# Cross, linear and one-head attention: the projection's tiles run inside the normalisation's block, each waiting for its chunk of 512 tokens

## Chip, cores and metric

One core of one Trainium2 chip runs the whole program. The metric is the device time of one execution in microseconds (us). TensorE is written PE, its weight loads PEld, VectorE DVE, ScalarE ACT, GpSimd POOL and SyncE SP.

## What is computed

Two decoder layers work on x of 2 x 1024 tokens x 256 features, each sublayer in the form `x = x + f(layernorm(x))`. The change touches the second, fourth and fifth of the six sublayers:

```
layernorm(x) = (x - mean(x)) / sqrt(var(x) + 1e-5)          # over the 256 features
x = x + cross(layernorm(x), ctx)      # 16 heads, q = xn @ Wq.T, k, v from 77 context rows per batch
x = x + linear(layernorm(x))          # q, k = relu(...), v; sum over tokens of k v, then q times that
x = x + one_head(layernorm(x), ctx)   # xp = relu(xn @ W.T + b), yp = relu(ctx @ W.T + b), softmax(xp yp), times ctx
```

All of it is float32.

## The kernel before

The 2048 tokens (N) lie along the free dimension and the 256 features on 128 partitions in C = 2 halves, so X and XN are tiles of 128 x 2 x 2048. Work on tokens goes in NCH = 4 chunks of W = 512. The kernel is a sequence of blocks. A block holds an instruction list for each engine; inside it engines wait only for each other's semaphores, and at its end all engines meet in a barrier, which the order below prints as two branches, the second of which waits for the release.

`norm` (L91) is one such block. PE multiplies a chunk by a matrix of 1/256 for the mean (L132, PSUM banks 0 to 3), DVE subtracts it (L152, signal `centred`), ACT squares (L184), PE forms the variance (L139, banks 4 to 7), ACT takes the reciprocal root with its square and its half (L188, L191, L193), DVE refines it (L159, signal `newton`, and L163, signal `rstd_ready`), and the chunk is scaled: chunks 0 and 1 by POOL (L225, signal `scaled`), 2 and 3 by DVE (L168, signal `scaled_dve`). The parameters of the sublayer are loaded by SP in the same block (signal `moved`).

`project` (L264) is a block that works through a list of `Tile`s: for tile n, PE sums the tile's products in bank n % 8 (L290, signal `summed`), and the tile's engine, ACT or DVE, takes the bank out to SBUF (L335, L339, L1756, L1881; signals `taken_act` and `taken_dve`). From the ninth tile on PE first waits until the tile eight places earlier has been taken. `steps` (L342) is a block for a chain of small operations, here fills of constants (L1275, L1769, L1870) and the two operations that make a mask (L1876, L1878).

The three sublayers `cross` (L1261), `linear` (L1738) and `cross_one` (L1858) each begin with `norm`, then have the projections of XN and the context in one `project`, in `cross` and `cross_one` with a block of `steps` between the two, in `linear` behind them. Cross has 14 tiles: 8 of q (512 columns, two products each), 4 of k (77 columns) and 2 of v. Linear has 16 pairs of k and v tiles (256 columns) and 8 of q. One-head has 8 tiles of xp (512 columns) and 2 of yp (154 columns). Each product appears in the trace as two matmul instructions.

Of the kernel before, what the change touches and what calls it, by code (L numbers as in the profile page):

```python
# [15 lines left out]
P = 128  # L16
B, T, D = 2, 1024, 256
N = B * T
# [25 lines left out]
class Signal:  # L44


    def __init__(self, sem):
        self.sem, self.base = sem, 0
# [39 lines left out]
    moved.passed(16 * len(pairs))  # L88


def norm(k, src, dst, centre=True, eps=EPS, weight=None, bias=None, loads=(), later=(), later_in=None, fills=()):  # L91

# [5 lines left out]
    var_ready, root_ready, root_squared = k.sig("var_ready"), k.sig("root_ready"), k.sig("root_squared")  # L98
    newton, halved, rstd_ready = k.sig("newton"), k.sig("halved"), k.sig("rstd_ready")
    scaled, scaled_dve, normed, filled = k.sig("scaled"), k.sig("scaled_dve"), k.sig("normed"), k.sig("filled")  # L100
    affine = weight is not None
    with ExitStack() as ctx:

# [74 lines left out]

        @block.scalar
        def _(act):  # L180
# [30 lines left out]
            if affine:  # L211
                for c in range(NCH):
                    affine_chunk(c)

        @block.gpsimd
        def _(pool):
# [24 lines left out]
    if loads:  # L241
        moved.passed(16 * len(loads))
    filled.passed(len(fills))


class Tile:

    def __init__(self, products, engine, take, rows=P, cols=W, then=None):  # L250
        self.products, self.engine, self.take, self.rows, self.cols = products, engine, take, rows, cols
        self.then = then


class Pending:
# [8 lines left out]
def project(k, tiles, banks=8, pending=None, beside=()):  # L264
# [15 lines left out]
    with nc.Block() as block:  # L280
# [53 lines left out]
def copy_to(dst, func=ACT.Copy, scale=1.0):  # L334
    return lambda eng, bank: eng.activation(dst, bank, func, scale=scale)  # L335
# [925 lines left out]
def cross(k, a):  # L1261

    X = k.X
    with ExitStack() as ctx:
        XN = k.sb("XN", [P, C, N], ctx=ctx)
        w = [k.sb(n, [P, C, D], ctx=ctx) for n in ("wq", "wk", "wv", "wo")]
        cx = k.sb("cx", [P, C, B * S2], ctx=ctx)
        norm(k, X, XN, loads=[(cx[:], a["ctx"])] + [(t[:], a["cross_" + n]) for t, n in zip(w, "qkvo")])
        recip = k.sb("recip", [P, B * CPB * C, W], ctx=ctx)
        jobs, tiles = [], []  # L1270
        for b in range(B):
            kk = k.sb("kk", [P, C, S2], ctx=ctx)
            v = k.sb("v", [P, 1, D], ctx=ctx)
            jobs.append(Job(k.sb("q", [P, C, T], ctx=ctx)[:], kk[:], v, X[:, :, b * T:(b + 1) * T]))
        steps(k, "chain", [("dve", lambda e, job=job: e.memset(job.v[:], 0.0)) for job in jobs])  # L1275
        for b, job in enumerate(jobs):
            for m in range(C):
                cols = slice(m * P, (m + 1) * P)
                for h in range(CPB):
                    prods = [(w[0][:, c, cols], XN[:, c, b * T + h * W:b * T + (h + 1) * W]) for c in range(C)]  # L1280
                    tiles.append(Tile(prods, "act", copy_to(job.q[:, m, h * W:(h + 1) * W])))
                prods = [(w[1][:, c, cols], cx[:, c, b * S2:(b + 1) * S2]) for c in range(C)]
# [455 lines left out]
def linear(k, a):  # L1738

    nc, ps, X = k.nc, k.ps, k.X  # L1740
    with ExitStack() as ctx:
# [5 lines left out]
        norm(k, X, XN, loads=[(w[:], a["lin_qkv"]), (wo[:], a["lin_proj"]), (bias[:], a["lin_bias"]),  # L1747
                              (same[:], a["same_head"])])
# [3 lines left out]
        vt = k.sb("lv", [P, N // P, D], ctx=ctx)  # L1752
        tiles = []
        for t in range(N // P):
            prods = [(XN[:, c, t * P:(t + 1) * P], w[:, c, D:3 * D]) for c in range(C)]
            tiles.append(Tile(prods, "act", lambda e, bank, t=t: e.activation(kt[:, t, 0:D], bank[:, 0:D], ACT.Relu)))  # L1756
            tiles.append(Tile([(XN[:, c, t * P:(t + 1) * P], w[:, c, 2 * D:3 * D]) for c in range(C)], "dve",
                              dve_copy_to(vt[:, t, :]), cols=D))
            tiles[-2].cols = D
            tiles[-2].products = [(l, r[:, 0:D]) for l, r in prods]  # L1760
# [7 lines left out]
        ones = k.sb("lones", [P, P], ctx=ctx)  # L1768
        steps(k, "chain", [("dve", lambda e: e.memset(ones[:], 1.0))])  # L1769
        tiles = []  # L1770
        for b in range(B):
            for c in range(C):
# [85 lines left out]
def cross_one(k, a):  # L1858
# [3 lines left out]
    with ExitStack() as ctx:  # L1862
# [5 lines left out]
        mask_in = k.sb("mask_in", [P, B, S2], I32, ctx=ctx)  # L1868
        mask = k.sb("mask", [P, B, S2], ctx=ctx)
        steps(k, "chain", [("dve", lambda e: e.memset(ct[:], 0.0))])  # L1870
        norm(k, X, XN, loads=[(w[:], a["one_w"]), (bias[:], a["one_bias"]), (cx[:], a["ctx"]),
                              (ct[0:S2, :, :], a["ctx_rows"])]
             + [(mask_in[:, b, :], a["mask"][b:b + 1, :].broadcast_to([P, S2])) for b in range(B)])
        yp = k.sb("yp", [P, C, B * S2], ctx=ctx)
        xp = k.sb("xp", [P, C, N], ctx=ctx)
        steps(k, "chain", [("dve", lambda e: e.tensor_copy(mask[:], mask_in[:])),  # L1876

                           ("dve", lambda e: e.tensor_scalar(mask[:], mask[:], -3e38, 10.0, ALU.mult, ALU.mult))])  # L1878
        tiles = []
        for m in range(C):  # L1880
            relu = lambda dst, m: (lambda e, bank: e.activation(dst, bank, ACT.Relu, bias=bias[:, m:m + 1]))  # L1881
            tiles.append(Tile([(w[:, c, m * P:(m + 1) * P], cx[:, c, :]) for c in range(C)], "act",
                              relu(yp[:, m, :], m), cols=B * S2))
            for h in range(NCH):
                prods = [(w[:, c, m * P:(m + 1) * P], XN[:, c, h * W:(h + 1) * W]) for c in range(C)]
                tiles.append(Tile(prods, "act", relu(xp[:, m, h * W:(h + 1) * W], m)))
# [5 lines left out]
        for h in range(NCH):  # L1892
            b = h // CPB
            for g in range(G):
# [4 lines left out]
        project(k, tiles)  # L1899
# [235 lines left out]
```

## Time and profile before

| | |
|---|---|
| time, median of 3 runs | 2994.42 us (2988.17 to 2995.18) |
| the profiled execution's own time | 2993.08 us |
| its span in the trace | 2990.6 us |
| granted PE clock, mean of the span | 0.923 of full speed |
| PE, DVE, ACT, POOL busy | 79%, 65%, 60%, 44% of the span |

The median is 1.34 us above the profiled execution, and the three runs lie within 7 us of each other. Busy shares are means over six sublayers with different limits; most of the span is the first sublayer. The three places that the change touches lie at 1555 to 1600 us (cross), 2641 to 2711 us (linear) and 2757 to 2800 us (one-head) of the span.

### The profile page before, as it was taken

What the parts mean: (1) busy time and instruction counts of PE and PEld (TensorE: products, weight loads), DVE (VectorE), ACT (ScalarE), POOL (GpSimd) and SP (SyncE); (2) the same over time, 40 slices, a digit from 0 to 9 for tenths busy, and PEclk for the clock granted to TensorE, in tenths of its full rate; (3) what the DMA queues carried; (4) which work ended last, traced back from release to release, by engine and by line L of the source; (5) the groups of instructions that cost most, each with busy time, mean ns of one, the idle gap of its engine ahead of it and who ended that gap; (6) DMA issues with size and microseconds to landing.
All of it is one profiled execution on the core that took longest, in us unless ns stands there. A gap on an engine that the chain in (4) does not pass through costs nothing. (4 is left out here: it accounts for less than half of the span.)

```text
span 2990.6 us, 38704 instructions
## 1 busy us (share of the span) xinstructions
PE 2374.3 (79%) x12420; PEld 1200.4 (40%) x12421; DVE 1957.9 (65%) x1762; ACT 1794.5 (60%) x2789; POOL 1311.3 (44%) x492
## 2 busy tenths in 40 slices
PE   5688888888868888888877667797787499868778
PEld 2344444444334444444435123223222355545333
DVE  4699999999669999999964657515913122233440
ACT  4799999999479999999951440270064211122330
POOL 2089998999508999999951110000000300020000
PEclk8899999999989999999996889898889699979889
DMA  2320001000133000100000400010012400010000
GB/s 77 90 76 28 25 29 39 28 25 28 41 88 77 28 25 29 39 28 28 25 20 3 113 36 1 9 40 11 1 34 88 174 21 21 20 43 9 28 0 28
DMA packets 59817, 116.17 MB, mean 39 GB/s; under 512 B 13619, under 2 KB 21811, under 8 KB 58304
## 3 DMA queue, kind: packets, MB, share of 16 engines
q1 hardware_dynamic: 51104, 103.72, 11.0%
q0 software_dynamic: 8608, 11.05, 1.3%
q8 instruction: 65, 1.06, 0.1%
q14 instruction: 40, 0.33, 0.0%
HBM read 86.92 MB, written 27.53 MB: 38 GB/s over the span
## 5 line engine op out<-in xcount | busy, mean ns | idle before, releaser
L838 POOL TENSOR_TENSOR hs<-hs,c_bc 128x2048 f32<-128x2048 f32 x256 | 1166.3, 4556 | 63.9 <-DVE hs L889 48.6
L889 DVE TENSOR_TENSOR_SCAN hs<-decays,ps 128x512 f32<-128x512 f32 x512 | 610.8, 1215 | 26.4 <-PE ps L916 8.0
L889 DVE TENSOR_TENSOR_SCAN hs<-decays,carry,ps 128x512 f32<-128x512 f32 x512 | 621.7, 1270 | 8.5 <-PE ps L916 7.7
L924 PE MATMUL ps<-hs,sel 128*64 128x512 f32 x2048 | 498.4, 608 | 15.4 <-POOL hs L838 15.1
L916 PE MATMUL ps<-ident,dbu_even 128*128 128x128 f32 x2048 | 294.9, 283 | 94.8 <-DVE hs L889 65.8
L916 PE MATMUL ps<-ident,dbu_odd 128*128 128x128 f32 x2048 | 294.9, 283 | 91.5 <-DVE hs L889 60.5
L852 ACT ACTIVATE decays<-delta_far,A 128x512 f32<-128x512 f32 x512 | 358.2, 712 | 10.3 <-DVE hs L889 10.2
L852 ACT ACTIVATE decays<-delta_near,A 128x512 f32<-128x512 f32 x512 | 356.4, 707 | 3.2 <-DVE hs L889 3.2
L860 ACT ACTIVATE dbu_odd<-du_turned,b_turned 128x512 f32<-128x512 f32 x512 | 357.1, 710 | 0.0
L860 ACT ACTIVATE dbu_even<-du_turned,b_turned 128x512 f32<-128x512 f32 x496 | 346.0, 710 | 0.0
L916 PEld LDWEIGHTS ps<-ident,dbu_odd 128*128 128x128 f32 x2048 | 221.1, 142 | 241.4 <-DVE hs L889 188.0
L916 PEld LDWEIGHTS ps<-ident,dbu_even 128*128 128x128 f32 x2048 | 219.0, 141 | 245.4 <-DVE hs L889 196.1
L1071 ACT ACTIVATE prob<-ps 128x1024 f32<-128x1024 f32 (+2 forms) x224 | 176.0, 837 | 161.5 <-PE ps L1042 137.5
L924 PEld LDWEIGHTS ps<-hs,sel 128*64 128x64 f32 x2048 | 124.6, 136 | 213.0 <-issue 186.4
L994 POOL DMA_DIRECT2D q<-o_rows x13 | 9.1, 698 | 401.5 <-DMA o_rows<-osb 336.8
L1196 PE MATMUL ps<-kx,qx 32*128 32x77 f32 (+4 forms) x1280 | 135.7, 545 | 55.9 <-DVE negmax L1223 33.0
L1080 DVE COPY osb<-ps 128x512 f32<-128x512 f32 x32 | 21.8, 690 | 215.3 <-PE ps L1053 213.3
L1223 DVE TENSOR_REDUCE negmax<-ps 128x4 f32<-128x2048 f32 (+4 forms) x70 | 138.8, 2028 | 22.6 <-PE ps L1201 14.9
L1627 PE MATMUL ps<-w_wv,x_turned 128*128 x304 | 141.2, 608 | 10.7 <-ACT x_turned L1686 10.7
L1722 DVE TENSOR_SCALAR hid_turned<-ps 128x512 f32<-128x512 f32 x38 | 26.3, 691 | 178.6 <-PE ps L1635 178.6
L1036 PE MATMUL ps<-qx,kx 32*128 32x512 f32 (+4 forms) x896 | 112.4, 572 | 38.7 <-PEq L1244 20.4
L1384 POOL DMA_INDIRECT rows<-ys,slot x16 | 15.2, 949 | 249.3 <-ACTq L1380 244.7
(260 smaller groups left out, 2664.3 us busy)
## 6 DMA issues: line engine op xcount, KB each, us to landing
c_bc<-c_rows SPq DMA_DIRECT2D x256, 128.0 KB, 2.8
o_rows<-osb SPq DMA_DIRECT2D x32, 256.0 KB
u_rows<-u SPq DMA_DIRECT2D x4, 1024.0 KB, 4.5
d_rows<-delta SPq DMA_DIRECT2D x4, 1024.0 KB, 4.2
delta_near<-d_rows SPq DMA_DIRECT2D x4, 1024.0 KB, 9.8
hs<-u_rows SPq DMA_DIRECT2D x4, 1024.0 KB, 6.5
delta_far<-d_rows SPq DMA_DIRECT2D x4, 1024.0 KB, 12.1
w_down<-in_expert_proj SPq DMA_DIRECT2D x1, 4096.0 KB, 36.6
```

The lines of the kernel that those rows point to most:

```text
L838: pool.tensor_tensor(x, x, spread(c_bc[:, g, :], 4), ALU.mult).then_inc(weighed.sem, 1)
L852: act.activation(decays[:, s % RING, :], (far if q else near)[:, blk, :], ACT.Exp, scale=A[:, at(i * GB, g), blk]).then_inc(decay.sem, 1)
L860: act.activation(dbu[0], dbu[1], ACT.Copy, scale=dbu[2]).then_inc(made.sem, 1)
L889: dve.tensor_tensor_scan(hs[:, quad % RING, n, :], decays[:, s % RING, :], ps[:, DBU + s % RING, :], carry[:, at(i * GB, g), blk] if q els ...
L916: mm = pe.transpose(ps[:, DBU + s % RING, t * P:(t + 1) * P], room[g % 2][:, t, blk, :, :].rearrange("p n d -> p (n d)"), k.ident[:])
L924: mm = pe.matmul(ps[lo:lo + DB, ACC + quad % 2 * 2 + j // 2, :], k.sel2[:, :], hs[:, quad % RING, j, :], start=False, stop=False, skip_gro ...
L1036: mm = pe.matmul(ps[0:krows, 2 * (m % 3) + j % 2, first:W], job.kx[rows, par, c, t * P:t * P + krows], job.qx[rows, par, c, qc * W + first ...
L1071: act.activation(prob[0:krows, m % 4, :, first:W], ps[0:krows, 2 * (m % 3):2 * (m % 3) + 2, first:W], ACT.Exp).then_inc(weighed.sem, 1)
L1196: mm = pe.matmul(ps[:, STRIPS * (f % 2) + j, at:at + m], qx[strip, par, c, t * P:(t + 1) * P], kx[strip, par, c, o:o + m], start=True, sto ...
L1223: dve.tensor_reduce(to[:, :, groups[0]:groups[0] + per], banks[:, :, :, 0:m], AX.X, ALU.max, negate=True).then_inc(maxed.sem, 1)
L1627: mm = pe.matmul(ps[:, 2 * h + g, :], xt[:, p, c, :], wv[:, bass.ds(e * (C * 2 * FF) + (c * 2 * FF + g * FF + h * HALF), HALF)], start=(c ...
L1722: dve.tensor_scalar(hid_t[:, h, :, :], ps[:, HID + h, :].rearrange("p (f n) -> p f n", f=HT), 1.0, None, ALU.mult).then_inc(hid_copied.sem, 1)
```

## The change

The list of tiles is handed to `norm`, whose block now also does what `project` did. Behind its last variance, PE goes through the tiles; each tile of XN waits for the signal that its chunk (`chunk=`) is scaled, and the first eight tiles wait until the bank of a mean or of a variance has been read. ACT and DVE take the tiles out at the end of their own part of the normalisation. The tiles are ordered by chunk, and those of the context stand last. The fills of constants move ahead of `norm`; the two mask operations of one-head move into the later `project` of the scores, as operations that DVE does `beside` it. The core of the diff:

```diff
@@ norm, PE, behind the last variance
+            if tiles:
+                pe.wait_ge(moved.sem, moved.at(16 * len(loads)))
+            for n, t in enumerate(tiles):
+                if n < NCH:
+                    if centre:
+                        pe.wait_ge(centred.sem, centred.at(n + 1))
+                elif n < 2 * NCH:
+                    pe.wait_ge(newton.sem, newton.at(n - NCH + 1))
+                else:
+                    old = n - 2 * NCH
+                    pe.wait_ge(taken[tiles[old].engine].sem, taken[tiles[old].engine].at(count[old]))
+                if t.chunk is not None:
+                    if affine:
+                        pe.wait_ge(normed.sem, normed.at((t.chunk + 1) * C))
+                    elif t.chunk < BY_POOL:
+                        pe.wait_ge(scaled.sem, scaled.at(t.chunk + 1))
+                    else:
+                        pe.wait_ge(scaled_dve.sem, scaled_dve.at(t.chunk - BY_POOL + 1))
+                multiply(pe, ps, t, n % 8).then_inc(summed.sem, 1)
@@ norm, DVE, behind the last chunk; ACT alike
+            take_tiles(dve, "dve", k, tiles, count)
+def take_tiles(eng, name, k, tiles, count):
+    summed, taken = k.sig("summed"), k.sig("taken_" + name)
+    for n, t in enumerate(tiles):
+        if t.engine == name:
+            eng.wait_ge(summed.sem, summed.at(n + 1))
+            t.take(eng, k.ps[0:t.rows, n % 8, 0:t.cols]).then_inc(taken.sem, 1)
@@ project, DVE
+            if beside:
+                dve.wait_ge(went_by.sem, went_by.at(len(beside)))
             take_all(dve, "dve")
@@ cross
-        norm(k, X, XN, loads=[(cx[:], a["ctx"])] + [(t[:], a["cross_" + n]) for t, n in zip(w, "qkvo")])
...
         steps(k, "chain", [("dve", lambda e, job=job: e.memset(job.v[:], 0.0)) for job in jobs])
         for b, job in enumerate(jobs):
+            for h in range(CPB):
+                for m in range(C):
+                    prods = [(w[0][:, c, m * P:(m + 1) * P], XN[:, c, b * T + h * W:b * T + (h + 1) * W])
+                             for c in range(C)]
+                    tiles.append(Tile(prods, "act", copy_to(job.q[:, m, h * W:(h + 1) * W]), chunk=b * CPB + h))
...
-        project(k, tiles)
+        norm(k, X, XN, loads=[(cx[:], a["ctx"])] + [(t[:], a["cross_" + n]) for t, n in zip(w, "qkvo")], tiles=tiles)
@@ linear
+        steps(k, "chain", [("dve", lambda e: e.memset(ones[:], 1.0))])
         tiles = []
...
         for h in range(NCH):
+            for t in range(h * W // P, (h + 1) * W // P):
+                x = [XN[:, c, t * P:(t + 1) * P] for c in range(C)]
+                tiles.append(Tile([(x[c], w[:, c, D:2 * D]) for c in range(C)], "act",
+                                  copy_to(kt[:, t, 0:D], ACT.Relu), cols=D, chunk=h))
+                tiles.append(Tile([(x[c], w[:, c, 2 * D:3 * D]) for c in range(C)], "dve",
+                                  dve_copy_to(vt[:, t, :]), cols=D, chunk=h))
             for m in range(C):
                 prods = [(w[:, c, m * P:(m + 1) * P], XN[:, c, h * W:(h + 1) * W]) for c in range(C)]
-                tiles.append(Tile(prods, "act", copy_to(q[:, m, h * W:(h + 1) * W], ACT.Relu)))
-        project(k, tiles)
+                tiles.append(Tile(prods, "act", copy_to(q[:, m, h * W:(h + 1) * W], ACT.Relu), chunk=h))
+        norm(k, X, XN, loads=[(w[:], a["lin_qkv"]), (wo[:], a["lin_proj"]), (bias[:], a["lin_bias"]),
+                              (same[:], a["same_head"])], tiles=tiles)
@@ cross_one
+        for h in range(NCH):
+            for m in range(C):
+                prods = [(w[:, c, m * P:(m + 1) * P], XN[:, c, h * W:(h + 1) * W]) for c in range(C)]
+                tiles.append(Tile(prods, "act", relu(xp[:, m, h * W:(h + 1) * W], m), chunk=h))
+        for m in range(C):
+            tiles.append(Tile([(w[:, c, m * P:(m + 1) * P], cx[:, c, :]) for c in range(C)], "act",
+                              relu(yp[:, m, :], m), cols=B * S2))
...
-        project(k, tiles)
+        project(k, tiles, beside=[lambda e: e.tensor_copy(mask[:], mask_in[:]),
+                                  lambda e: e.tensor_scalar(mask[:], mask[:], -3e38, 10.0, ALU.mult, ALU.mult)])
```

What this does to PE's list in cross, where the normalisation ends and the projection begins, before the change (a row is one or more products; L139 is the variance, L290 a tile's product, and a signal in brackets is what the row waits for):

```order
L139 MATMUL ps<-norm_sq,inv 128x512 [waits squared]
L139 MATMUL ps<-norm_sq,inv 128x512
L230 UNCONDITIONAL_BRANCH
L281 UNCONDITIONAL_BRANCH [waits barrier_Pool_Activation_PE_DVE_SP_release]
L290 MATMUL ps<-XN,wq 128x512 x4
L290 MATMUL ps<-cx,wk 128x77 x2
L290 MATMUL ps<-XN,wq 128x512 x4
L290 MATMUL ps<-cx,wk 128x77 x2
```

And the same place of PE's list with the change (L141 is now the variance, L298 a tile's product):

```order
L141 MATMUL ps<-norm_sq,inv 128x512 [waits squared]
L141 MATMUL ps<-norm_sq,inv 128x512
L298 MATMUL ps<-XN,wq 128x512 [waits scaled,centred,moved]
L298 MATMUL ps<-XN,wq 128x512
L298 MATMUL ps<-XN,wq 128x512 [waits scaled,centred]
L298 MATMUL ps<-XN,wq 128x512
```

The two branches of the barrier are gone, and the first products of q follow the last variance; tiles 0 to 7 now carry two or three waits where they carried none.

In linear, PE's list around the ninth tile is this with the change (w_qkv,XN are tiles of k and v, XN,w_qkv those of q; the first two rows are the eighth tile, the third and fourth the ninth):

```order
L298 MATMUL ps<-w_qkv,XN 128x256 [waits scaled,newton]
L298 MATMUL ps<-w_qkv,XN 128x256
L298 MATMUL ps<-XN,w_qkv 128x512 [waits scaled,taken_act]
L298 MATMUL ps<-XN,w_qkv 128x512
L298 MATMUL ps<-XN,w_qkv 128x512 [waits scaled,taken_dve]
L298 MATMUL ps<-XN,w_qkv 128x512
L298 MATMUL ps<-w_qkv,XN 128x256 [waits scaled,taken_act]
L298 MATMUL ps<-w_qkv,XN 128x256
```

The tiles of q, which stood behind all of k and v, now stand behind each chunk's own, and from the ninth tile on PE waits for takes that ACT and DVE do only after their part of the normalisation.

On DVE the scores' block of one-head begins with the mask operations (L1953, L1954), ahead of the first score (L1951):

```order
L1953 CAST mask_192<-mask_in_191 128x154
L1954 TENSOR_SCALAR mask_192<-mask_192 128x154 [waits went_by]
L1951 TENSOR_TENSOR sc_200<-ps,mask_192 128x77 [waits summed,went_by]
L1951 TENSOR_TENSOR sc_200<-ps,mask_192 128x77 [waits summed] x15
```

Before, the two stood in a block of their own between the normalisation and the projection.

## Rows read from the trace of the kernel before

**Rows 1.** Timeline, around the cross projection: start us, us, engine, line, operation [idle before it <- releaser]
```profile
1554.50 0.69 DVE L1258 TENSOR_TENSOR X<-X,ps 128x512 f32<-128x512 f32 x1 [2.74 <-PE ps L290]
1555.82 3.67 PE L132 MATMUL ps<-X,inv 128*128 128x512 f32 x8 [1.35 <-PEq L280]
...
1569.71 1.98 PE L139 MATMUL ps<-norm_sq,inv 128*128 128x512 f32 x4 [0.69 <-ACT norm_sq L184]
...
1569.97 2.35 POOL L225 TENSOR_TENSOR XN<-XN,norm_rstd 128x1024 f32<-128x1024 f32 x1 [1.08 <-DVE norm_rstd L163]
...
1575.49 1.23 DVE L168 TENSOR_TENSOR XN<-XN,norm_rstd 128x1024 f32<-128x1024 f32 x1
1577.12 0.66 DVE L1275 MEMSET v<- 128x256 f32 x2 [0.40 <-PEq L230]
...
1578.32 6.41 PE L290 MATMUL ps<-XN,wq 128*128 128x512 f32 x8 [6.63 <-PEq L345]
```

**Rows 2.** Timeline, around the linear projection
```profile
2640.68 1.22 DVE L1403 TENSOR_TENSOR X<-X,ps 128x1024 f32<-128x1024 f32 x1 [3.75 <-PE ps L1394]
...
2642.22 5.24 PE L132 MATMUL ps<-X,inv 128*128 128x512 f32 x8 [1.58 <-PEq L1380]
...
2663.48 1.23 DVE L168 TENSOR_TENSOR XN<-XN,norm_rstd 128x1024 f32<-128x1024 f32 x1
2665.00 29.59 PEld L290 LDWEIGHTS ps<-w_qkv,XN 128*128 128x128 f32 x128 [6.15 <-issue]
2665.03 29.96 PE L290 MATMUL ps<-w_qkv,XN 128*128 128x256 f32 x128 [5.35 <-PEq L230]
...
2707.05 0.60 ACT L335 ACTIVATE lq<-ps 128x512 f32<-128x512 f32 x1 [1.12 <-PE ps L290]
...
2708.76 0.60 ACT L335 ACTIVATE lq<-ps 128x512 f32<-128x512 f32 x1 [1.12 <-PE ps L290]
...
2710.39 1.86 PEld L290 LDWEIGHTS ps<-lv,lk 128*128 128x128 f32 x16 [2.49 <-issue]
```

**Rows 3.** Timeline, around the one-head projection
```profile
2757.82 0.48 DVE L1870 MEMSET ct<- 128x512 f32 x1 [0.46 <-PEq L1788]
...
2758.85 3.67 PE L132 MATMUL ps<-X,inv 128*128 128x512 f32 x8 [2.27 <-PEq L345]
...
2780.34 0.24 DVE L1878 TENSOR_SCALAR mask<-mask 128x154 f32<-128x154 f32 x1
...
2781.11 1.36 PE L290 MATMUL ps<-cx,w_one 128*128 128x154 f32 x4 [6.39 <-PEq L345]
...
2782.51 0.39 ACT L1881 ACTIVATE yp<-ps,one_bias 128x154 f32<-128x154 f32 x1 [5.74 <-PE ps L290]
...
2798.26 0.69 ACT L1881 ACTIVATE xp<-ps,one_bias 128x512 f32<-128x512 f32 x1 [1.03 <-PE ps L290]
...
2799.25 7.34 PE L290 MATMUL ps<-yp,xp 128*128 128x77 f32 x64 [1.03 <-PEq L280]
2799.93 0.24 DVE L1897 TENSOR_TENSOR sc<-ps,mask 128x77 f32<-128x77 f32 x1 [19.35 <-PE ps L290]
```

**Rows 4.** Windows: stretch, us, busy us of each engine, granted clock, DMA share, GB/s
```profile
1555.80:1571.70 15.90, 14.51 (x32) 5.82 (x32) 8.16 (x9) 11.31 (x15) 4.08 (x2) 1.00 0.24 77
1578.30:1584.60 6.30, 6.28 (x9) 2.72 (x10) 0.00 (x0) 0.60 (x1) 0.00 (x0) 0.56 0.00 0
1584.60:1599.20 14.60, 13.86 (x49) 7.31 (x47) 1.80 (x6) 4.18 (x7) 0.00 (x0) 1.00 0.00 0
2665.00:2669.50 4.50, 4.47 (x11) 3.68 (x12) 0.42 (x1) 0.38 (x1) 0.00 (x0) 0.52 0.02 4
2669.50:2709.40 39.90, 39.22 (x151) 28.17 (x149) 6.36 (x15) 10.54 (x23) 0.00 (x0) 1.00 0.00 0
2781.10:2785.60 4.50, 4.49 (x9) 2.60 (x10) 0.00 (x0) 0.39 (x1) 0.00 (x0) 0.53 0.00 0
2785.60:2799.20 13.60, 12.62 (x33) 5.57 (x31) 0.00 (x0) 5.78 (x9) 0.00 (x0) 1.00 0.00 0
```

More of the change, by code:

```diff
@@ L88, in load, with norm @@
     moved.passed(16 * len(pairs))
-def norm(k, src, dst, centre=True, eps=EPS, weight=None, bias=None, loads=(), later=(), later_in=None, fills=()):
+def norm(k, src, dst, centre=True, eps=EPS, weight=None, bias=None, loads=(), later=(), later_in=None, fills=(),
+         tiles=()):
     nc, ps = k.nc, k.ps
@@ L100, in norm @@
     scaled, scaled_dve, normed, filled = k.sig("scaled"), k.sig("scaled_dve"), k.sig("normed"), k.sig("filled")
+    summed, taken, done, count = k.sig("summed"), signals_taken(k), *takes_of(tiles)
     affine = weight is not None
@@ L213, in _ @@
                     affine_chunk(c)
+            take_tiles(act, "act", k, tiles, count)
         @block.gpsimd
@@ L243, in norm, with __init__, signals_taken, takes_of @@
     filled.passed(len(fills))
+    summed.passed(len(tiles))
+    for name in taken:
+        taken[name].passed(done[name])
 class Tile:
-    def __init__(self, products, engine, take, rows=P, cols=W, then=None):
+    def __init__(self, products, engine, take, rows=P, cols=W, then=None, chunk=None):
         self.products, self.engine, self.take, self.rows, self.cols = products, engine, take, rows, cols
-        self.then = then
+        self.then, self.chunk = then, chunk
+def signals_taken(k):
+    return {"act": k.sig("taken_act"), "dve": k.sig("taken_dve")}
+def takes_of(tiles):
+    done = {"act": 0, "dve": 0}
+    count = []
+    for t in tiles:
+        done[t.engine] += 1
+        count.append(done[t.engine])
+    return done, count
+def multiply(pe, ps, t, bank):
+    for i, (lhs, rhs) in enumerate(t.products):
+        mm = pe.matmul(ps[0:t.rows, bank, 0:t.cols], lhs, rhs, start=(i == 0), stop=(i == len(t.products) - 1))
+    return mm
+def take_tiles(eng, name, k, tiles, count):
[4 more added lines that the diff above has]
+            t.take(eng, k.ps[0:t.rows, n % 8, 0:t.cols]).then_inc(taken.sem, 1)
 class Pending:
@@ L1276, in cross @@
         for b, job in enumerate(jobs):
-            for m in range(C):
[L1278 to L1282, printed above, removed]
+            for h in range(CPB):
[3 more added lines that the diff above has]
+                    tiles.append(Tile(prods, "act", copy_to(job.q[:, m, h * W:(h + 1) * W]), chunk=b * CPB + h))
+        for b, job in enumerate(jobs):
+            for m in range(C):
+                prods = [(w[1][:, c, m * P:(m + 1) * P], cx[:, c, b * S2:(b + 1) * S2]) for c in range(C)]
                 tiles.append(Tile(prods, "dve", dve_copy_to(job.kk[:, m, :]), cols=S2))
@@ L1746, in linear @@
         same = k.sb("same_head", [P, P], ctx=ctx)
-        norm(k, X, XN, loads=[(w[:], a["lin_qkv"]), (wo[:], a["lin_proj"]), (bias[:], a["lin_bias"]),
-                              (same[:], a["same_head"])])
         q = k.sb("lq", [P, C, N], ctx=ctx)
@@ L1752, in linear @@
         vt = k.sb("lv", [P, N // P, D], ctx=ctx)
+        ones = k.sb("lones", [P, P], ctx=ctx)
+        steps(k, "chain", [("dve", lambda e: e.memset(ones[:], 1.0))])
         tiles = []
[L1754 to L1760, printed above, removed]
-        for h in range(NCH):
+        for h in range(NCH):
+            for t in range(h * W // P, (h + 1) * W // P):
[4 more added lines that the diff above has]
+                                  dve_copy_to(vt[:, t, :]), cols=D, chunk=h))
             for m in range(C):
                 prods = [(w[:, c, m * P:(m + 1) * P], XN[:, c, h * W:(h + 1) * W]) for c in range(C)]
-                tiles.append(Tile(prods, "act", copy_to(q[:, m, h * W:(h + 1) * W], ACT.Relu)))
-        project(k, tiles)
+                tiles.append(Tile(prods, "act", copy_to(q[:, m, h * W:(h + 1) * W], ACT.Relu), chunk=h))
+        norm(k, X, XN, loads=[(w[:], a["lin_qkv"]), (wo[:], a["lin_proj"]), (bias[:], a["lin_bias"]),
+                              (same[:], a["same_head"])], tiles=tiles)
         ctxw = k.sb("ctxw", [P, B, C, P], ctx=ctx)
         ksw = k.sb("ksw", [P, B, C, P], ctx=ctx)
-        ones = k.sb("lones", [P, P], ctx=ctx)
-        steps(k, "chain", [("dve", lambda e: e.memset(ones[:], 1.0))])
         tiles = []
@@ L1870, in cross_one @@
         steps(k, "chain", [("dve", lambda e: e.memset(ct[:], 0.0))])
+        yp = k.sb("yp", [P, C, B * S2], ctx=ctx)
+        xp = k.sb("xp", [P, C, N], ctx=ctx)
+        relu = lambda dst, m: (lambda e, bank: e.activation(dst, bank, ACT.Relu, bias=bias[:, m:m + 1]))
+        tiles = []
+        for h in range(NCH):
[5 more added lines that the diff above has]
+                              relu(yp[:, m, :], m), cols=B * S2))
         norm(k, X, XN, loads=[(w[:], a["one_w"]), (bias[:], a["one_bias"]), (cx[:], a["ctx"]),
                               (ct[0:S2, :, :], a["ctx_rows"])]
[L1873 to L1886, printed above, removed]
-        project(k, tiles)
+             + [(mask_in[:, b, :], a["mask"][b:b + 1, :].broadcast_to([P, S2])) for b in range(B)], tiles=tiles)
         sc = k.sb("sc", [P, NCH, G, S2], ctx=ctx)
@@ L1898, in cross_one @@
                     sc[:, h, g, :], bank, mask[:, b, :], ALU.add), cols=S2))
-        project(k, tiles)
+        project(k, tiles, beside=[lambda e: e.tensor_copy(mask[:], mask_in[:]),
+                                  lambda e: e.tensor_scalar(mask[:], mask[:], -3e38, 10.0, ALU.mult, ALU.mult)])
         flat = sc[:].rearrange("p h g s -> p (h g) s")
```

## The prediction

> **What bounds the kernel now.** The busy shares of the page say little here, since they are a mean over six sublayers and the change touches some 160 us of 2990.6. I read the timeline around the three places first, then the windows, for the clock granted there. In each of the three the order is the same: PE ends the last variance, the normalisation's small operations on ACT, DVE and POOL go on, a barrier and in two of the three a block of fills or mask operations follow, and PE stands until the first tile. In cross PE's last variance begins at 1569.71 and ends 1.98 us later, at 1571.69; the next PE row is the first product of q at 1578.32, with 6.63 us idle before it [rows 1]. In linear the pause is 5.35 us [rows 2], in one-head 6.39 us [rows 3]. No other engine does anything in these pauses that the tiles need from outside the normalisation.
>
> After each pause the windows show the second loss: the granted clock is 0.56 over the first 6.30 us of the tiles in cross, 0.52 over the first 4.50 us in linear and 0.53 over 4.50 us in one-head, and 1.00 behind that. 0.5 is the lower of the two levels, 1.2 GHz, and 1.00 the upper, 2.4 GHz. Inside the cross normalisation, where PE is busy 14.51 of 15.90 us, the clock is 1.00 [rows 4].
>
> During the tiles PE is what everybody waits for: ACT waits 1.12 us for each q tile of linear and works 0.60 us, so a tile comes every 1.71 us (2707.05 to 2708.76) [rows 2].
>
> **What the change does, part by part.** *The pause.* With the change the first tile stands behind the last variance. Is its chunk ready by then? In cross, POOL's second chunk is scaled from 1569.97 to 1572.32 [rows 1]; it began 1.08 us after POOL's first chunk had ended, at 1568.89, so chunk 0 is ready 2.8 us before PE gets to tile 0 at 1571.69. At 1.71 us for a tile of 512 columns, PE comes to chunk 1 at 1575.1 (ready 1572.32) and to chunk 3, 6 x 1.71 us behind the start, at 1581.9; DVE's last scaling ends at 1576.72 [rows 1]. One-head runs the same normalisation with the same operations. In linear a chunk is eight tiles of 256 columns and two of 512, 10.3 us, so chunks are never waited for. Nothing else is late: all three pauses go. That is 6.63 + 5.35 + 6.39 = 18.4 us.
>
> *The banks.* Tile 7 waits for `newton` of chunk 3, which DVE gives before it begins its last scaling. In linear that begins at 2663.48 at the latest; PE, which would start at 2665.03 - 5.35 = 2659.68, has seven tiles of 0.86 us (half of 1.71) ahead of tile 7 and reaches it at 2665.7. Tile 9 is the first that needs a take of DVE, and DVE is free at 2663.48 + 1.23 = 2664.71 [rows 2], so tile 1 is taken by 2665.2; PE gets to tile 9 at 2659.68 + 8 x 0.86 + 1.71 = 2668.3. The slack is 2 to 3 us at each. This is where a small error would turn into a new wait, since a DVE instruction that waits there has all later v tiles queued behind it.
>
> *The ramp.* If PE goes on without a pause, the tiles begin at full clock. The lower clock now costs 6.30 x (1 - 0.56) = 2.77 us, 4.50 x 0.48 = 2.16 us and 4.50 x 0.47 = 2.12 us [rows 4], together 7.05 us.
>
> *The waits themselves.* Up to 56 tiles (8 in cross, 40 in linear, 8 in one-head) now carry two or three waits. In linear the tiles from the ninth on already carry one, for a take. The 128 weight loads of this stretch stand in one row of 29.59 us beside 29.96 us of PE, with no idle between them [rows 2], so one wait that is already satisfied costs nothing. Two or three the trace does not show next to each other with their signals long up. Lower bound 0; upper bound a weight load that is no longer loaded ahead, 29.59 / 128 = 0.23 us for each of 56 tiles, 13 us. I take 0, as the nearest row is the one with a single wait.
>
> *The fills that move ahead.* In one-head a fill already stands ahead of the norm: 0.46 us, the fill's 0.48 us, and PE starts 0.55 us later [rows 3]. Without one, PE starts 0.63 us behind DVE's last addition in cross (1555.19 to 1555.82) and 0.32 us in linear (2641.90 to 2642.22) [rows 1, 2]. So cross gets 0.46 + 0.66 + 0.55 - 0.63 = 1.04 us longer, 0.66 being the two fills of v, and linear, whose fill is a quarter of one-head's (I take 0.17 us as in proportion to 0.66 for 512 columns), 0.46 + 0.17 + 0.55 - 0.32 = 0.86 us. In linear the fill leaves its old place: from the last take's end at 2709.36 to the next weight load at 2710.39 are 1.03 us; a bare change of blocks takes 0.30 us (2798.95 to 2799.25 in one-head) [rows 2, 3], so 0.73 us come back. Cross's and one-head's old blocks lie within the pauses and are counted there. The net is 1.04 + 0.86 - 0.73 = 1.2 us of loss. The pause of PE ahead of the norm grows in cross from 1.35 us to about 2.4 us. One-head has 2.27 us there and its eight products still take 3.67 us, as in cross now; linear, which starts at the lower clock, takes 5.24 us [rows 1 to 3]. I count nothing, and 1.6 us as the upper bound.
>
> *The order of tiles.* PE's products are the same in number and size, in other order. In one-head the last take is now a yp of 0.39 us in place of an xp of 0.69 us [rows 3], 0.3 us gained. The mask operations, 0.24 us each, lie at the head of DVE's part of the scores' block; that begins at about 2799.2 and the first score comes at 2799.93 [rows 3], so they end with 0.2 us to spare. Without that cover they would cost 0.5 us. The added wait in the last sublayer's `project` stands where DVE has no tiles to take, so nobody is behind it.
>
> **The sum.** 18.4 + 7.05 - 1.2 + 0.3 = 24.6 us: 8.4 in cross, 7.4 in linear, 8.8 in one-head. The profiled execution took 2993.08 us, so 2968.5; the median of the runs is 1.34 us above the profiled one, so by it 2969.8. I say 2969. What follows each place (the maxima in cross, the sums in linear, the scores in one-head) begins with data that these tiles make, and with no load, so it moves forward whole.
>
> **The rivals.** *The ramp stays.* The clock falls at the turn from variances to tiles, or the tiles' first products start on the lower level as they do now. For it: the tiles have always begun there. Against it: they began behind a pause of 5 us or more, and inside the norm the clock stays 1.00 through idle stretches like the 0.69 us before the last variance [rows 1, 4]. It would give 2993.1 - (24.6 - 7.05) = 2975.5 us.
>
> *The tiles do not start early.* Something in the norm that I take as done is not, and PE waits until DVE's last scaling has ended in each place, and starts cold. Then only the block changes are saved: 1578.32 - 1576.72 = 1.6 us in cross, 0.32 us in linear (2664.71 to 2665.03), 1.4 us in one-head (from 0.6 us ahead of the second mask operation, where the block begins, to 2781.11 [rows 3]), plus the 0.3, less the 1.2: about 2.4 us, 2990.7 us. Against it stand the 2 to 3 us of slack at each wait.
>
> *Slower: the clock of the tiles.* The whole of the tiles' work, now in closer company with the norm's and in turn with waits for banks, is granted the lower clock in part. At full clock it is 14.60 + 39.90 + 13.60 us and 0.56, 0.52 and 0.53 of the stretches at the lower one (3.5 + 2.3 + 2.4), 76.4 us [rows 4]. Every tenth of it at half speed costs 7.6 us; from 32% on, 24.6 us are eaten and the kernel is slower; all of it would give 2968.5 + 76.4 = 3044.9 us. Against it: linear's tiles already wait for banks from the ninth on, and their 39.90 us are granted 1.00 with PE busy 39.22 [rows 4]. The Trainium skill, page "TensorE: Matmul & The Clock Gate", section "A second HAM failure mode: psum-queue depth-cycling", speaks for this rival: a kernel that cycles through the PSUM banks and leaves PE idle a little between groups of matmuls was seen to go back and forth between the two clocks. By the page the sum would come out on the slower side if a third of the tiles were hit, by the rows it stays 24.6 us; the trace does not agree with the page for this cycle of eight banks.
>
> *The waits cost.* At the upper bound 13 us are lost: 2981.5 us, still faster.
>
> **How the numbers follow.** Forecast as computed 0.80; the ramp stays 0.09; the waits cost most of their bound 0.03; the tiles do not start early 0.05; slower by the clock 0.03. A measurement of this kernel can tell about 0.3%, 9 us, from no change. Faster by more than that are the first three, 0.92; within it the fourth, 0.05; slower the last, 0.03. The range has to hold the first two cases: down to 2961, as the three runs of before reach 6 us under their median and the last product of a tile may overlap the next better than the rows' modelled ends say; up to 2979, the ramp at 2975.5 with the 1.6 us of a cold start in cross and some of the waits.
>
> **What would show it.** Right: a first tile (L298) of each place within 0.5 us of the end of the last variance (L141), at a granted clock of 1.00 in the first 5 us of tiles; PE without idle over 0.3 us between tiles; the next block at 8 to 9 us less behind the start of the sublayer than now. Wrong: PE rows of L298 with idle before them released by POOL XN, DVE XN or a take; a window of tiles at a clock under 0.9; a pause or a lower clock in the cross norm's first products; a first score waiting for DVE's mask.

## The result, and the profile after

The changed kernel takes 2967.49 us (median of 4 runs, 2965.65 to 2973.16), the kernel before 2994.14 us over its 4 runs by now. The ratio is 0.9914 with a 95% interval of 0.9901 to 0.9928: 0.86% less, which is 25.7 us (the two medians lie 26.65 us apart). The forecast was 2969 us, within 2961 to 2979.

The cross sublayer in the timeline of the changed kernel (L134 is the mean, L141 the variance, L298 a tile's product, L248 and L189 the scaling by POOL and DVE, L393 and L397 the takes; columns as in [rows 1]):

```profile
1556.55 0.66 DVE L1332 MEMSET v<- 128x256 f32 x2 [0.71 <-PEq L336]
...
1557.75 5.06 PE L134 MATMUL ps<-X,inv 128*128 128x512 f32 x8 [2.64 <-PEq L403]
...
1573.03 1.98 PE L141 MATMUL ps<-norm_sq,inv 128*128 128x512 f32 x4 [0.69 <-ACT norm_sq L206]
1573.30 2.36 POOL L248 TENSOR_TENSOR XN<-XN,norm_rstd 128x1024 f32<-128x1024 f32 x1 [1.08 <-DVE norm_rstd L184]
...
1574.85 13.90 PE L298 MATMUL ps<-XN,wq 128*128 128x512 f32 x32
...
1578.48 0.60 ACT L393 ACTIVATE q<-ps 128x512 f32<-128x512 f32 x1 [0.94 <-PE ps L298]
1578.82 1.23 DVE L189 TENSOR_TENSOR XN<-XN,norm_rstd 128x1024 f32<-128x1024 f32 x1
...
1592.93 2.00 ACT L1220 ACTIVATE qx<-q,heads 128x2048 f32<-128x2048 f32 x1 [3.55 <-PEq L253]
```

The last variance begins at 1573.03 and the first tile at 1574.85, with no idle in brackets: the 6.63 us of [rows 1] are gone. All 32 matmuls of q, two for each product, stand in one row of 13.90 us, 0.43 us each, so neither a wait for a chunk nor two or three waits on a tile cost PE anything. DVE's last scaling begins when PE is at its third tile. ACT takes the tiles with 1.12 us of waiting between them, as it did before. But the eight first matmuls of the norm take 5.06 us where they took 3.67, which the forecast had priced at nothing, with 1.6 us as the upper bound.

Linear, in the same columns:

```profile
2633.21 6.63 PE L134 MATMUL ps<-X,inv 128*128 128x512 f32 x8 [2.33 <-PEq L403]
...
2650.93 7.07 PE L298 MATMUL ps<-w_qkv,XN 128*128 128x256 f32 x32
...
2654.89 1.22 DVE L189 TENSOR_TENSOR XN<-XN,norm_rstd 128x1024 f32<-128x1024 f32 x1
...
2656.04 1.08 DVE L397 COPY lv<-ps 128x256 f32<-128x256 f32 x3
...
2657.83 3.60 PE L298 MATMUL ps<-XN,w_qkv 128*128 128x512 f32 x8
...
2692.49 0.60 ACT L393 ACTIVATE lq<-ps 128x512 f32<-128x512 f32 x1 [1.12 <-PE ps L298]
2693.36 1.86 PEld L346 LDWEIGHTS ps<-lv,lk 128*128 128x128 f32 x16 [1.74 <-issue]
```

DVE comes out of the normalisation late and takes three banks of v one behind the other (x3, 2656.04); PE, whose tile 9 (the second of q) needs the first of them, is at its q tiles only from 2657.83 and does not wait. One-head:

```profile
2741.82 5.24 PE L134 MATMUL ps<-X,inv 128*128 128x512 f32 x8 [2.28 <-PEq L403]
...
2759.10 13.90 PE L298 MATMUL ps<-XN,w_one 128*128 128x512 f32 x32
...
2774.78 0.24 DVE L1953 CAST mask<-mask_in 128x154 f32<-128x154 int32 x1 [10.48 <-PEq L253]
2774.78 7.34 PE L346 MATMUL ps<-yp,xp 128*128 128x77 f32 x64 [0.73 <-PEq L253]
2775.05 0.24 DVE L1954 TENSOR_SCALAR mask<-mask 128x154 f32<-128x154 f32 x1
2775.53 0.61 DVE L1951 TENSOR_TENSOR sc<-ps,mask 128x77 f32<-128x77 f32 x2 [0.23 <-PE ps L346]
```

The mask operations end at 2775.29 and DVE still waits 0.23 us for the first scores; they are covered. The windows give the clock (columns as in [rows 4]), the starts of the norms first and third and fifth, the tiles between them:

```profile
1557.70:1561.10 3.40, 3.35 (x5) 1.59 (x6) 0.00 (x0) 1.49 (x2) 0.00 (x0) 0.58 0.61 183
1574.80:1588.60 13.80, 13.80 (x34) 6.09 (x33) 5.11 (x6) 6.09 (x11) 0.86 (x1) 1.00 0.01 1
2633.20:2637.00 3.80, 3.79 (x5) 1.73 (x6) 0.00 (x0) 1.46 (x2) 0.00 (x0) 0.50 0.73 230
2650.90:2692.50 41.60, 41.55 (x161) 30.21 (x159) 11.59 (x22) 12.23 (x28) 0.83 (x1) 1.00 0.00 0
2741.80:2745.40 3.60, 3.58 (x5) 1.68 (x6) 0.02 (x1) 0.20 (x1) 0.00 (x0) 0.56 0.55 141
2759.10:2774.00 14.90, 14.90 (x41) 7.06 (x39) 5.06 (x6) 7.64 (x13) 0.80 (x1) 1.00 0.00 0
```

The tiles have the upper clock from the first on in all three places, PE busy without a gap. The lower clock has come up at the norms instead, in linear as before, in cross and one-head anew. In one-head that was not to be expected: none of its instructions ahead of the norm was changed, and PE's pause there is 2.28 us against 2.27 us in [rows 3].

To compare kernels without the rest of the program I use one length for each place: from the end of DVE's last addition ahead of the norm to the first instruction of the block behind the tiles; in linear to the first product of lv and lk, so that the block of the fill that used to stand there is counted. Worked out from the timelines (us; the medians are of each kernel's own runs). One of the twelve executions of e2 took 4660.82 us and is left out of its median.

| kernel | cross | linear | one-head | sum | median |
|---|---|---|---|---|---|
| before | 44.03 | 68.52 | 41.89 | 154.44 | 2994.14 |
| changed | 37.09 | 61.26 | 34.45 | 132.80 | 2967.49 |
| e1, changed, again | 35.70 | 61.27 | 32.88 | 129.85 | 2969.18 |
| e2, tiles wait for all chunks | 44.65 | 68.24 | 41.12 | 154.01 | 2988.03 |
| e3, before, PE kept busy | 41.28 | 66.42 | 40.56 | 148.26 | 2988.00 |
| e4, cross only | 35.71 | 68.54 | 42.05 | 146.30 | 2985.57 |
| e5, linear only | 44.06 | 61.17 | 42.27 | 147.50 | 2985.99 |
| e6, one-head only | 43.71 | 68.54 | 32.88 | 145.13 | 2981.81 |
| e7, order of tiles of before | 35.70 | 61.22 | 32.87 | 129.79 | 2969.59 |
| e8, fills by POOL | 34.42 | 60.02 | 31.72 | 126.16 | 2964.98 |
| e9, changed, third time | 35.70 | 61.23 | 32.87 | 129.80 | 2969.59 |
| e10, e8 again | 34.43 | 60.07 | 31.71 | 126.21 | 2964.03 |

In the first trace of the changed kernel the three places give 21.6 us and the span is 26.7 us shorter; the other 5.1 us came from outside them. Of these, 2.2 us lie behind the scores of one-head, where the product with ct starts at once on the upper clock and before did not:

```profile
2821.97 9.25 PE L290 MATMUL ps<-pt,ct 128*128 128x512 f32 x16 [0.94 <-PEq L1911]
2797.38 7.11 PE L346 MATMUL ps<-pt,ct 128*128 128x512 f32 x16 [0.94 <-PEq L1966]
```

The first row is the kernel before, the second the changed one. Their first 5 us are granted 0.56 and 1.00 of the clock, with the same instructions and the same 0.94 us of idle ahead.

### The profile page after: what moved, and what is told of

It reads as the page before. It is cut to its first block and busy times, and to the rows that moved or that the text cites. A ratio compares the mean times of both kernels' runs of the same rounds, so it can differ in the third digit from the quotient of the medians.

```text
span 2963.9 us, 38715 instructions
## 1 busy us (share of the span) xinstructions
PE 2368.1 (80%) x12420; PEld 1195.6 (40%) x12421; DVE 1957.6 (66%) x1762; ACT 1794.0 (61%) x2789; POOL 1311.3 (44%) x492
## 5 line engine op out<-in xcount | busy, mean ns | idle before, releaser
L982 PE MATMUL ps<-hs,sel 128*64 128x512 f32 x2048 | 498.4, 608 | 15.5 <-POOL hs L896 15.3
```

Source lines behind the costliest of these rows:

```text
L982: mm = pe.matmul(ps[lo:lo + DB, ACC + quad % 2 * 2 + j // 2, :], k.sel2[:, :], hs[:, quad % RING, j, :], start=False, stop=False, skip_gro ...
```

## The experiments

**e1 and e9: the changed kernel again.** No edit.

> The changed kernel once more. In its first trace the eight first products of the norm took 5.06, 6.63 and 5.24 us in cross, linear and one-head, where before they took 3.67, 5.24 and 3.67: the lower clock is gone at the tiles and has come up at the norms. If that belongs to where the pauses of PE lie in this program, the three read the same again, and the time is 2966 to 2970 us. If it is chance, one of the three at least reads otherwise, 3.67 us where it was 5.06 or 5.24, and the time moves by about 1.5 us for each.

> The changed kernel a third time, beside e10, to set the two against each other on one chip. By the two traces so far the three places take 21.6 and 24.6 us less than before, the difference being the lower clock at the norms of cross and one-head in the first (centring of chunk 0 3.4 and 3.6 us behind PE's start, against 2.0). If that is chance, this trace shows 2.0 or about 3.5 us in each of the two, independent of the other, and 35.7 or 37.1 us for cross, 32.9 or 34.5 us for one-head, 61.3 us for linear. 2966 to 2970 us.

2969.18 us and 2969.59 us, ratios 0.9920 (0.9907 to 0.9932) and 0.9912 (0.9898 to 0.9925). The times are where both expectations had them. The timeline of e1 at the norms of cross and of one-head:

```profile
1559.44 3.67 PE L134 MATMUL ps<-X,inv 128*128 128x512 f32 x8 [2.63 <-PEq L403]
...
1561.43 1.22 DVE L173 TENSOR_TENSOR XN<-X,ps 128x1024 f32<-128x1024 f32 x1 [2.53 <-PE ps L134]
...
2747.66 3.67 PE L134 MATMUL ps<-X,inv 128*128 128x512 f32 x8 [2.27 <-PEq L403]
```

The eight matmuls are back at 3.67 us in both places, behind the same pauses. In cross the mean is subtracted from the first chunk (it is centred) from 1561.43 on, 1.99 us behind PE's start at 1559.44, where the first trace had 3.38 us. So the first branch of the expectation for e1, that the lower clock belongs to this program at these two places, is wrong: it comes and goes between executions of one and the same kernel. e9 shows the upper clock in both again. With it the three places give 24.6 us in both repeats.

**e2: every tile of XN waits for the whole normalisation.**

```diff
-                    elif t.chunk < BY_POOL:
-                        pe.wait_ge(scaled.sem, scaled.at(t.chunk + 1))
                     else:
-                        pe.wait_ge(scaled_dve.sem, scaled_dve.at(t.chunk - BY_POOL + 1))
+                        pe.wait_ge(scaled.sem, scaled.at(BY_POOL))
+                        pe.wait_ge(scaled_dve.sem, scaled_dve.at(NCH - BY_POOL))
```

> The changed kernel, except that each tile of XN waits for the whole normalisation and not for its chunk; blocks, fills and orders stay. If the early start is what pays, PE stands again for about 5.0 us behind each last variance, the tiles begin at the lower clock, and some 15 + 7 us come back: 2987 to 2993 us. If it is the block less in each place (the barrier and the loading of the next block's instructions) that pays, it stays within 5 us of the changed kernel, 2966 to 2972 us.

2988.03 us, ratio 0.9985 (0.9976 to 0.9994). The timeline of e2 in cross, and the window of its first tiles:

```profile
1572.71 1.98 PE L141 MATMUL ps<-norm_sq,inv 128*128 128x512 f32 x4 [0.69 <-ACT norm_sq L205]
...
1578.48 1.22 DVE L188 TENSOR_TENSOR XN<-XN,norm_rstd 128x1024 f32<-128x1024 f32 x1
1579.85 6.66 PE L297 MATMUL ps<-XN,wq 128*128 128x512 f32 x10 [5.16 <-DVE XN L188]
```

```profile
1579.80:1584.80 5.00, 4.95 (x7) 2.21 (x8) 0.00 (x0) 0.60 (x1) 0.00 (x0) 0.57 0.00 0
```

PE stands 5.16 us for DVE's last scaling and begins at 0.57 of the clock. Against e1, the same kernel with the wait for a chunk, the three places are 24.2 us longer: 16.0 us of pauses (5.16, 5.18 and 5.17 us, and the 0.16 us by which e1's tiles begin ahead of the modelled end of the last variance), 6.8 us between the first tile and the next block, and 1.4 us for the lower clock at the norm of cross, which came up in this trace. The wait for a chunk is thus worth 22.8 us of the 24.6.

Against the kernel before, the three places are only 0.4 us shorter, 1.8 us without the lower clock at the norm of cross. That is not the price of the blocks alone: the pauses are 2.9 us shorter than before, and PE starts 2.0 us later because of the fills ahead of the norms. The forecast's rival "the tiles do not start early" had 2.4 us for this case. The median is 5.8 us under that of its own comparison, 4.5 us by the ratio, with an interval of 1.8 to 7.2 us. In its trace 2.7 us lie outside the places, 2.4 us of them at the product with ct behind one-head's scores, as above; whether that is so in the other executions is not known.

**e3: the kernel before, PE kept busy in part of the pause.** Five products (ten matmuls) behind each last variance go into a bank that nobody reads any more; they compute nothing that is used.

```diff
@@ norm, PE, behind the last variance; spin=5 in the three sublayers
+            for _ in range(spin):
+                pe.matmul(ps[:, 0, :], k.inv[:, :], src[:, 0, 0:W], start=True, stop=True)
```

> The kernel before, except that PE does five more products of 512 columns behind each of the three last variances, into a bank that nobody reads any more; nothing starts earlier. It prices the ramp alone. If the clock at the tiles is worth what the windows say, the tiles' first 5 us read 1.00 and 7.05 us are saved at the most: 2986 to 2989 us. If the lower clock only moves to the next pause of PE, the tiles read 1.00 but less than 4 us are saved: 2990 to 2994 us. If five products don't hold the clock over the 1 to 2.3 us of pause that is left, the tiles' first stretch reads near 0.55 again and nothing is saved.

2988.00 us, ratio 0.9979 (0.9970 to 0.9988), 5.8 us less. The timeline of e3 in cross (L148 are the added products), and the windows of the first tiles in the three places:

```profile
1569.48 4.45 PE L148 MATMUL ps<-X,inv 128*128 128x512 f32 x10
...
1576.27 3.67 PE L292 MATMUL ps<-XN,wq 128*128 128x512 f32 x8 [2.34 <-PEq L347]
```

```profile
1576.20:1581.20 5.00, 4.93 (x15) 2.56 (x16) 0.24 (x1) 1.19 (x2) 0.00 (x0) 1.00 0.00 0
2660.20:2665.20 5.00, 5.00 (x23) 4.43 (x24) 0.85 (x2) 1.16 (x3) 0.00 (x0) 1.00 0.00 0
2775.20:2780.20 5.00, 5.00 (x15) 2.44 (x15) 0.00 (x0) 1.77 (x3) 0.00 (x0) 1.00 0.00 0
```

The first eight matmuls of q take 3.67 us, against 6.41 us in [rows 1], at the upper clock, although they begin as late behind the norm's start as before (22.50 us). Tile start to next block is 18.16 us in cross against 20.90, 43.29 against 45.39 in linear, 16.05 against 18.14 in one-head: 2.74 + 2.10 + 2.09 = 6.9 us. That is the ramp alone, 7.05 us in the forecast, and it shows that the lower clock at the tiles came from PE's standing and not from the tiles. One-head gives 0.8 us back at its norm, whose first eight matmuls took 5.37 us in this trace.

**e4, e5, e6: one sublayer alone.** Each is the changed kernel with the other two sublayers' functions of before.

> Only cross is changed, linear and one-head are as before. By the prediction 8.4 us are saved, 2985.7 us. By the trace of the changed kernel the stretch from the last addition before the norm to the first operation behind the tiles is shorter by 6.9 us, 1.4 us of the predicted gain having gone into the lower clock at the norm: 2987.2 us. Were there something that only pays with all three together, less than 5 us would be saved.

> Only linear is changed, cross and one-head are as before. By the prediction 7.4 us are saved, by the trace of the changed kernel 7.3: 2986 to 2988 us. A new wait for a bank (tile 7 for the last refinement, tile 9 for a take of DVE) would show as idle of PE before L298 and a saving under 6 us.

> Only one-head is changed, cross and linear are as before. By the prediction 8.8 us are saved, 2985.3 us; by the trace of the changed kernel 7.4 us, the first eight products of its norm having taken 5.24 in place of 3.67 us. Nothing ahead of that norm is changed, neither its own fill nor the pause of 2.3 us. If the lower clock there comes from where the program stands in time, it can be absent here, and 8.8 us are saved; if it comes from the change in one-head itself it is there, and 7.4 us are saved.

Cross alone 2985.57 us (ratio 0.9973, 0.9963 to 0.9983), its place 35.71 us, 8.3 us less. Linear alone 2985.99 us (0.9976, 0.9966 to 0.9985), its place 61.17 us, 7.4 us less (7.35). One-head alone 2981.81 us (0.9962, 0.9949 to 0.9976), its place 32.88 us, 9.0 us less. The three places sum to 24.7 us, as in the kernel with all three: each gain stands for itself, and none hangs on another. The medians sum to 28.4 us against their own comparisons; with intervals of 3 to 4 us on either side of each ratio that is no contradiction. Most of the excess is one-head's, 12.2 us by the median for 9.0 us in its place; its trace has the quick product with ct, 1.7 us, too. In linear of e5 the time from the first tile to the next block is 42.47 us, in e1 42.46 us, so the new waits for a bank cost nothing with linear changed alone either.

**e7: the tiles in the order of before.** Each tile still waits for its own chunk. In cross and linear:

```diff
         for b, job in enumerate(jobs):
-            for h in range(CPB):
-                for m in range(C):
+            for m in range(C):
+                for h in range(CPB):
...
-        for b, job in enumerate(jobs):
-            for m in range(C):
@@ linear
+        for h in range(NCH):
             for m in range(C):
                 prods = [(w[:, c, m * P:(m + 1) * P], XN[:, c, h * W:(h + 1) * W]) for c in range(C)]
```

> The changed kernel with the order of tiles of before in cross and linear (q, k and v of a batch by halves; all k and v, then q), each tile still waiting for its own chunk. By the slack in the trace no tile reaches PE before its chunk is scaled: in cross the second tile, chunk 1, would come at 1576.6 and POOL has scaled it by 1575.7. So the order is worth nothing, within 1 us of the changed kernel. If ordering by chunk matters, PE shows idle released by POOL XN or DVE XN, and 1 us or more is lost for each.

2969.59 us, ratio 0.9919 (0.9905 to 0.9932), as expected; the three places 129.79 us, as in e1. The timeline of e7 in cross:

```profile
1571.72 2.36 POOL L248 TENSOR_TENSOR XN<-XN,norm_rstd 128x1024 f32<-128x1024 f32 x1 [1.07 <-DVE norm_rstd L184]
1573.28 3.60 PE L298 MATMUL ps<-XN,wq 128*128 128x512 f32 x8
```

Two tiles, of chunks 0 and 1, stand in one row of 3.60 us. The second begins at 1575.0 and POOL has chunk 1 ready at 1574.08, so even this order leaves 0.9 us. Sorting the tiles by chunk is worth nothing here; that each waits for its own is what counts.

**e8 and e10: the fills move into the norm's block, on POOL.** In one-head the load that writes over part of the fill comes last of the loads and waits for it (`held=1`). The calls are shown in short.

```diff
@@ norm, SP
+                for n, (to, source) in enumerate(loads):
+                    if held and n == len(loads) - held:
+                        sp.wait_ge(filled.sem, filled.at(len(fills)))
+                    sp.dma_start(to, source).then_inc(moved.sem, 16)
@@ cross, linear and cross_one
-        steps(k, "chain", [("dve", lambda e, job=job: e.memset(job.v[:], 0.0)) for job in jobs])
-        steps(k, "chain", [("dve", lambda e: e.memset(ones[:], 1.0))])
-        steps(k, "chain", [("dve", lambda e: e.memset(ct[:], 0.0))])
+        norm(..., tiles=tiles, fills=[(job.v[:], 0.0) for job in jobs])
+        norm(..., tiles=tiles, fills=[(ones[:], 1.0)])
+        norm(..., tiles=tiles, fills=[(ct[:], 0.0)], held=1)
```

> The changed kernel without the three blocks of fills ahead of the norms: POOL does them at the head of the norm's own block, and in one-head the load of the context rows waits for its fill. In the changed kernel PE starts 1.91, 1.08 and 1.49 us behind DVE's last addition; without a block of fills it should be about 0.6, 0.3 and 0.6 us, 3.0 us saved. With shorter pauses of PE the lower clock at the norms may also go, 1.4 us in each of cross and one-head. So 2 to 6 us below the changed kernel: 2962 to 2966 us. If the fills delay POOL's scaling or the loads, PE shows idle before its first tile.

> The kernel of e8 again. By its first trace the three places take 34.4, 60.0 and 31.7 us, 3.7 us less than the changed kernel at the same clock; where the pause ahead of the norm is 1.35 us or less no trace has yet shown the lower clock at the norm, so the three should read the same again within 0.2 us. 3 to 5 us under e9.

2964.98 us (ratio 0.9900, 0.9885 to 0.9915) and 2964.03 us (0.9902, 0.9887 to 0.9917). The timeline of e8 at one-head's norm:

```profile
2747.55 0.75 DVE L1903 SCALAR_TENSOR_TENSOR X<-ps,lbias,X 128x512 f32<-128x512 f32 x1 [0.97 <-PE ps L1864]
...
2748.59 0.53 POOL L244 MEMSET ct<- 128x512 f32 x1 [90.25 <-POOLq L1846]
2748.62 3.67 PE L136 MATMUL ps<-X,inv 128*128 128x512 f32 x8 [1.11 <-PEq L1846]
```

PE starts 0.32 us behind DVE's addition in place of 1.49, and the fill runs on POOL beside it. The three places take 126.2 us in both traces, 3.6 us less than e1 and e9, where 3.0 us were expected. PE starts 1.28, 0.75 and 1.17 us earlier, 3.2 us; the other 0.4 us come at the norm of linear, where the lower clock ends earlier (the last variance begins 15.4 to 15.5 us behind PE's start in place of 15.9). In the medians e10 is 5.6 us under e9 on the same chip, for which 3 to 5 us were expected, but the intervals of the two ratios overlap; that it is faster than the changed kernel is shown by the places in four traces, not by the times. By the median it is the fastest version here. It also shows how much the rest of the program wanders: the profiled executions of e8 and e10 have the same length in the three places and spans of 2972.4 and 2960.4 us, at a mean clock of 0.919 and 0.927.

## Why the prediction was right

Its sum was 24.6 us in the three places, 8.4, 7.4 and 8.8. With cross and one-head at the norm's clock that it assumed, e1 gives 8.3, 7.3 and 9.0 us, 24.6 in all, and e1's and e9's medians are 24.6 us under their own comparisons. Term by term, before against e1:

- *The pause*, forecast 18.4 us. The tile begins 0.16 us ahead of the modelled end of the last variance in place of 6.63, 5.36 and 6.39 us behind it: 18.9 us. The forecast had placed this 0.16 us in the range. e2 shows that most of it is the wait until everything is scaled: with the blocks joined and that wait kept, 15.5 of the 18.4 us remain.
- *The ramp*, 2.77 + 2.16 + 2.12 = 7.05 us. From the first tile to the next block: 20.90 to 18.08 us in cross, 2.82; in linear 45.39 to 42.46, 2.93, of which 0.76 is the block of the fill that left (1.03 us in [rows 2], 0.27 us now); in one-head 18.14 to 15.68, 2.46, of which 0.30 is the smaller last take [rows 3]. That leaves 2.8 + 2.2 + 2.2. e3 has it alone, 6.9 us.
- *The waits*, 0 between 0 and 13 us: 0. PE is busy 41.55 of 41.60 us in linear's tiles, 40 tiles with two or three waits each.
- *The fills ahead*, 1.04 + 0.86 us. PE starts 1.91 us behind the addition in cross, 1.28 us later than before, since the block change ahead of the fill took 0.71 us and not one-head's 0.46; in linear 1.08 us, 0.76 us later. Together 2.04 for 1.90 us.
- *The pause ahead of linear's norm*, forecast at nothing: its norm starts at the lower clock as before and stays there longer (eight products 6.63 us, 5.24 in [rows 2]), but most of it is absorbed, and the last variance ends 0.44 us later.
- *The clock at cross's norm*, nothing with an upper bound of 1.6 us: 1.4 us in the first trace and in e2, nothing in e1, e4, e7 and e9. The bound was set for the pause that grows in cross; one-head lost 1.6 us in the first trace with its pause unchanged, for which the forecast had no term.
- *The order of tiles and the mask*, 0.3 us and nothing: so measured, and e7 finds no price in the order.

Of the signs that it named, one of being wrong appeared in the first trace: the lower clock in the first matmuls of cross's norm. And one of being right did not: the next block was to come 8 to 9 us sooner in each place, and came 6.9, 7.3 and 7.4 us sooner in the first trace and in linear 7.3 to 7.4 us in e1, e5, e7 and e9 too; for linear the forecast's own sum had 7.4 us. The other signs came as named.

None of the rivals came in. The tiles' clock is 1.00 in the windows of all three places, so the slower rival is not seen. The Trainium skill, page "TensorE: Matmul & The Clock Gate", section "A second HAM failure mode: psum-queue depth-cycling", describes a bf16 kernel in which PE is idle for short times between its groups of matmuls; here 40 float32 tiles of linear cycle through the eight banks with PE busy 41.55 of 41.60 us, so those short idles did not arise. No run here tests the page's case, and the prediction, which had 0.68 us of idle in 39.90 us to go by, said more than that shows where it let the trace disagree with the page. "The ramp stays" did not come at the tiles. In the first trace 3.0 us went to the lower clock at the norms of cross and one-head, in e1 and e9 nothing.

That 2967.49 us lies only 1.5 us under the forecast is in part luck. The first trace has 21.6 us from the three places and 5.1 us from outside them; e1 has 24.6 us from the places and loses 2.3 us outside.

## What to carry to other kernels

When one block ends in a chain of small operations and the next begins with work that needs only its first part, look at which chunk is ready when the waiting engine comes free: here the first was ready 2.8 us ahead, and PE stood for the later chunks, the barrier and, in two of three places, a block of small operations. Count a pause of PE with what the windows show behind it: here 18.4 us of standing cost 7 us more of products at half speed. A fill in a block of its own cost 0.8 to 1.3 us here, the fill included; give it to an engine that idles in a neighbouring block, as e8 does.

## What was not expected of the hardware

Behind a pause of PE of 2.3 to 2.6 us the norm's first matmuls came at the upper clock in most traces and at the lower in some, with the same instructions ahead. Of the 16 places with such a pause (cross with its fills ahead in 6 traces, one-head with its own in 10) 4 had it: the first chunk was centred 2.5 to 3.6 us behind PE's start in place of 2.0. Where the pause was 1.1 to 1.35 us none of 8 had. That is suggestive and no more: at one in four, eight in a row without it come about one time in ten. Linear is not among these places: its norm began at the lower clock in all 12 traces, behind pauses of 1.58 and 2.33 us alike. There the clock is 0.50 already ahead of the pause, with PE busy 2.53 of 7.50 us and then 1.93 of 3.10 us in the kernel before. Behind pauses of 5.2 to 6.6 us the tiles began at 0.50 to 0.66 in all 12 windows.

The product with ct in one-head is another such place. Behind 10.8 us of standing PE does its 16 small matmuls of sc at 0.50 to 0.56 and stands 0.94 us; then the 16 matmuls of pt and ct took 7.10 to 7.11 us in 4 traces (the first of the changed kernel, e1, e2 and e6) and 8.90 to 9.34 us in the other 8. All 4 are traces with one-head changed, but so are 4 of the 8; whether the change has a part in it is not shown.

Such differences add up over a program of 3 ms: between traces, what lies outside the three places varied from 5.1 us less than before to some 10 us more (e8), with hardly an instruction changed there (the mask operations of one-head and one wait). A change of 3 us is therefore read from its own stretch of the timeline and hardly from the time of the program.
